# Router products taken from the centred rows, ahead of the variance, in two FFN stages of a fused graph and mixture kernel

## The reference, cut to what matters

```python
def _layernorm(x, axis=-1, eps=1e-05):
    m = jnp.mean(x, axis=axis, keepdims=True)
    v = jnp.var(x, axis=axis, keepdims=True)
    return (x - m) / jnp.sqrt(v + eps)

x = x + _L0_gnn_ref(_layernorm(x), adj, adj, ...)        # attention over the graph, two GRU cells
x = x + _L0_ffn_ref(_layernorm(x)[None], ...)[0]         # shared expert + 8 routed experts, hidden 512, gelu
x = x + _L1_gnn_ref(_layernorm(x), adj, ...)             # bilinear features, adj @ x, relu
x = x + _L1_ffn_ref(_layernorm(x)[None], ...)[0]         # 8 routed experts, hidden 256, relu

# the router of the two FFN layers (first: softmax over all, then renormalised over the two best)
gate_logits = x_flat @ Wg + bg + bias
topk_vals, topk_idx = jax.lax.top_k(gate_logits, 2)
topk_w = jax.nn.softmax(topk_vals, axis=-1)
combine = (jax.nn.one_hot(topk_idx, 8) * topk_w[..., None]).sum(axis=1)
h = relu(einsum('td,edh->teh', x_flat, W1) + b1)
y = einsum('teh,ehd->ted', h, W2) + b2
out = einsum('ted,te->td', y, combine)
```

## Time and profile before

| | us |
|---|---|
| median of 3 runs | 2084.09 |
| the profiled execution's own time | 2085.21 |
| its span, first to last instruction | 2083.4 |
| TensorE busy | 1826.9 (88%) |
| VectorE busy | 1648.8 (79%) |
| ScalarE busy | 1337.1 (64%) |
| GpSimd busy | 221.5 (11%) |
| mean granted TensorE clock | 0.917 |

### The profile page before, as it was taken

How to read it: one execution, slowest core, us unless ns; L and a number is a source line. 1 busy time by engine, 2 the same in 40 slices (tenths; PEclk the granted TensorE clock), 3 DMA queues, 4 the chain that set the end, 5 groups by cost and what they waited for, 6 DMA issues and landing times.

```text
span 2083.4 us, 28364 instructions
## 1 busy us (share of the span) xinstructions
PE 1826.9 (88%) x9108; PEld 875.5 (42%) x9108; DVE 1648.8 (79%) x1393; ACT 1337.1 (64%) x1428; POOL 221.5 (11%) x163
## 2 busy tenths in 40 slices
PE   2511697999999999999998899999999989998997
PEld 2511342444444444444446344444444334455443
DVE  7645777988988998989567687878768988856998
ACT  4766136887887887888234556565546876735775
POOL 2000201000101011000441000000006910000000
PEclk6555798999999999999996999999998999988999
DMA  8998038555555556455500211111002079912321
GB/s 332 407 428 295 24 109 259 152 151 172 151 153 177 148 151 182 137 152 152 206 0 0 94 51 40 50 40 51 1 21 121 0 285 429 422 73 84 112 102 69
DMA packets 89852, 311.84 MB, mean 150 GB/s; under 512 B 15017, under 2 KB 52361, under 8 KB 79903
## 3 DMA queue, kind: packets, MB, share of 16 engines
q1 hardware_dynamic: 89778, 310.88, 42.4%
HBM read 297.88 MB, written 12.98 MB: 149 GB/s over the span
## 4 chain that ended last, share of the span: by engine, by line
PE 53%; DVE 3%; ACT 2%; issue 1%; POOL 0%; ACTq 0%; DVEq 0%; POOLq 0%
PE psum L1119 13%; PE psum L1131 13%; PE psum L1204 8%; PE psum L1067 8%; PE psum L1182 2%; PE psum L1092 1%; PE psum L1094 1%; PE psum L896 1%; PE psum L891 1%; PE psum L1106 1%; DVE prod L1727 1%; PE psum L902 1%; PE psum L1097 1%; PE psum L1096 1%; PE psum L1144 1%
## 5 line engine op out<-in xcount | busy, mean ns | idle before, releaser
L722 ACT ACTIVATE ss<-KR,cls 128x1024 bf16<-128x1024 int16 x384 | 413.0, 1138 | 106.4 <-DVE pl L1562 106.4
L1067 PE MATMUL psum<-ph,Tt 128*128 128x512 bf16 x1536 | 416.4, 380 | 6.7 <-DVE pl L1562 6.7
L800 ACT ACTIVATE hid<-psum,fB 128x1024 f32<-128x1024 f32 x208 | 227.4, 1112 | 184.3 <-PE psum L1119 184.2
L1119 PE MATMUL psum<-hTp,fW 128*128 (+1 forms) x1248 | 290.1, 383 | 7.7 <-ACT hid L800 3.8
L1131 PE MATMUL psum<-hidp,fW 128*128 128x512 bf16 x1248 | 280.1, 379 | 1.9 <-DVEq L1693 1.9
L1559 DVE TENSOR_TENSOR ph<-ss,Ahi 128x3072 bf16<-128x3072 bf16 x128 | 228.6, 1786 | 54.8 <-PE psum L1067 54.7
L1671 DVE TENSOR_TENSOR hidp<-hid,hidp 128x1024 bf16<-128x1024 f32 x208 | 245.5, 1222 | 26.6 <-ACT hidp L794 26.0
L1067 PEld LDWEIGHTS psum<-ph,Tt 128*128 128x128 bf16 x1536 | 149.9, 98 | 190.5 <-DVE pl L1562 7.1
L1067 PE MATMUL psum<-pl,Tt 128*128 128x512 bf16 x768 | 228.9, 380 | 0.0
L1562 DVE TENSOR_TENSOR pl<-ss,Alo 128x3072 bf16<-128x3072 bf16 x128 | 227.3, 1776 | 0.0
L1119 PEld LDWEIGHTS psum<-hTp,fW 128*128 128x128 bf16 x1248 | 117.2, 98 | 169.1 <-ACT hid L800 31.8
(11 more groups left out here) (231 smaller groups left out, 2131.4 us busy)
## 6 DMA issues: line engine op xcount, KB each, us to landing
Ar<-in_adjT SPq DMA_DIRECT2D x32, 2048.0 KB, 13.2
Ab<-in_adjT SPq DMA_DIRECT2D x128, 512.0 KB, 3.9
A<-in_adjT SPq DMA_DIRECT2D x32, 2048.0 KB, 10.1
mB<-mk_d SPq DMA_DIRECT2D x64, 512.0 KB, 3.7
Tt<-T_d SPq DMA_DIRECT2D x128, 192.0 KB, 2.3
Tt<-Tn_d SPq DMA_DIRECT2D x128, 64.0 KB, 2.1
T_d<-tb SPq DMA_DIRECT2D x32, 192.0 KB, 1.9
RD<-rden_d SPq DMA_DIRECT2D x12, 512.0 KB, 4.8
```

Source lines behind the costliest of these rows:

```text
L722: last = nc.scalar.activation(ss[s % 2][:, h, :], KR[:, h, rb * RB:(rb + 1) * RB], ACT.Sigmoid, scale=STEP, bias=cls[:, ds(t * HEADS + h, 1)])
L800: nc.scalar.activation(hid[j % HB][:, :], flat[:, j % 2 * CW:j % 2 * CW + CW], func, bias=fB1[:, j:j + 1]).then_inc(act_done[k], 1)
L1067: last = nc.tensor.matmul(psum[:, 2 * h + q, :], Tt[s % AS][:, h, w, :], mv[:, q * CH:(q + 1) * CH], start=fresh and k == 0, stop=False, s ...
L1119: last = nc.tensor.matmul(psum[:, j % 2 * 2 + b, :], fW[0][x][:, j * P:(j + 1) * P], hTp[y][:, ds(q * CW + b * CH, CH)], start=(w == 0), s ...
```

## The change

- TensorE no longer takes the router products from the scaled rows (`hT`) behind the 32 transposes. It takes them from the centred rows (`hc`), in bank 1 of PSUM. In the first stage the products of chunks 0 to 5 stand behind seven of the eight mean products, and those of chunks 6 and 7 between the variance products of chunks 3 and 4. In the second stage chunks 0 to 3 stand behind the mean products, chunks 4 to 7 between the variance products of chunks 3 and 4.
- VectorE multiplies the logits by the row factor right behind the Newton step (one new instruction of 128x256). The two bias additions follow the scaling of all rows.
- VectorE scales four chunks, forms the low halves of the first two, scales the other four, then goes to the selection. The low halves of chunks 2 to 7 stand behind those of the first hidden blocks. TensorE's first up products wait for four scaled chunks and two low halves, its main loop for all low halves.
- ScalarE takes the exponential behind two of the four first activations, not behind all four.

```diff
@@ lt_tensor
+            def routed(chunks):
+                pe.wait_ge(r_in, 96 * (k // 2 + 1))
+                for q in chunks:
+                    pe.wait_ge(lt_centred, NC * k + max(q, 1) + 1)
+                    for t in range(4 * q, 4 * q + 4):
+                        last = nc.tensor.matmul(psum[:, 1, NE * t:NE * t + NE], hc[:, t * P:(t + 1) * P], Wr[:, :],
+                                                start=(t == 0), stop=True, skip_group_check=True)
+                if q == NC - 1:
+                    last.then_inc(r_ps, 1)
             for q in range(NC):
                 if k == 0:
                     pe.wait_ge(g_nin, 2 * NC + (1 if q < 4 else 2))
                     pe.wait_ge(g_used, 2 * q + 4)
                 if k == 2:
                     pe.wait_ge(l_add, q + 1)
+                if k == 0 and q == NC - 1:
+                    routed(range(6))
                 nc.tensor.matmul(psum[:, q, :], mean, xT[:, q * CH:(q + 1) * CH], start=True,
                                  stop=True).then_inc(lt_mean, 1)
+            if k == 2:
+                routed(range(4))
             for q in range(NC):
+                if q == 4 and k != 1:
+                    routed(range((4, 0, 6)[2 - k], NC))
                 pe.wait_ge(lt_squared, NC * k + q + 1)
...
             for t in range(NT):
+                if t == 4 and k != 1:
+                    pe.wait_ge(r_sel, 3 * (k // 2) + 1)
@@ ffn_tensor
-                pe.wait_ge(r_in, 96 * (k + 1))
-                for t in range(NT):
-                    if t % 4 == 0:
-                        pe.wait_ge(ln_done, 3 + NC * 2 * k + t // 4)
-                    last = nc.tensor.matmul(psum[:, 0, NE * t:NE * t + NE], hT[:, t * P:(t + 1) * P], Wr[:, :],
-                                            start=(t == 0), stop=True, skip_group_check=True)
-                last.then_inc(r_ps, 1)
                 pe.sem_inc(down_done[k], hold)
-                pe.wait_ge(f_lo, (NC + 2) * (k + 1))
+                pe.wait_ge(ln_done, 2 + NC * 2 * k + 4)
+                pe.wait_ge(f_lo, (NC + 2) * k + 4)
...
-                pe.wait_ge(r_sel, 3 * k + 1)
                 for e in range(lag):
                     up(0, e)
+                pe.wait_ge(ln_done, 2 + NC * 2 * k + NC)
...
                 pe.wait_ge(r_mk8, 4 * k + 4)
+                pe.wait_ge(f_lo, (NC + 2) * (k + 1))
@@ lt_vector, k = 0 and 2
+                V.tensor_tensor(lg[:, :, :], psum[:, 1, 0:NT * NE].rearrange("p (t e) -> p t e", e=NE),
+                                stat[:, 4, :].unsqueeze(2).to_broadcast([P, NT, NE]), ALU.mult).then_inc(r_sel, 1)
+                for q in range(4):
+                    scaled(q)
+                for q in range(2):
+                    low_rows(f, q)
+                for q in range(4, NC):
+                    scaled(q)
```

More of the change, by code:

```diff
@@ L805, in hidden @@
                             high(q, j)
-                for j in range(HB):
+                for j in range(2):
                     hidden(0, j)
@@ L810, in ffn_scalar @@
                 nc.scalar.activation(rs[:, 3, :], rs[:, 2, :], ACT.Exp).then_inc(r_exp, 1)
+                for j in range(2, HB):
+                    hidden(0, j)
                 for b in range(4):
@@ L1288, in lt_vector, with scaled @@
                 inverse_root(slice(0, NT)).then_inc(ln_normed, 1)
-                for q in range(NC):
+                def scaled(q):
                     xq = slice(q * CH, (q + 1) * CH)
@@ L1292, in lt_vector, with low_rows @@
                     V.tensor_tensor(hT[:, xq], hc[:, xq], psum[:, q, :], ALU.mult).then_inc(ln_done, 1)
+                if k == 1:
+                    for q in range(NC):
+                        scaled(q)
+                    return
+                f = k // 2
+                dve.wait_ge(r_ps, f + 1)
+                dve.wait_ge(ln_normed, 3 + k)
+                V.tensor_tensor(lg[:, :, :], psum[:, 1, 0:NT * NE].rearrange("p (t e) -> p t e", e=NE),
[5 more added lines that the diff above has]
+                for q in range(4, NC):
+                    scaled(q)
+            def low_rows(k, q):
+                c_q = slice(q * CH, (q + 1) * CH)
+                dve.wait_ge(fh_hi, NC * k + q + 1)
+                V.tensor_tensor(hTp[1][:, c_q], hT[:, c_q], hTp[0][:, c_q], ALU.subtract).then_inc(f_lo, 1)
             dve.wait_ge(cst_in, 16)
@@ L1626, in ffn_vector @@
                 dve.sem_inc(hid_lo[k], HB)
[L1627 to L1634, removed]
                 dve.wait_ge(r_sel, 3 * k + 1)
+                c.link(V.tensor_tensor(lg[:, :, :], lg[:, :, :], rb2[:, 0, :].unsqueeze(1).to_broadcast(T), ALU.add))
                 c.link(V.tensor_tensor(lg[:, :, :], lg[:, :, :], rb2[:, 1, :].unsqueeze(1).to_broadcast(T), ALU.add))
@@ L1704, in ffn_vector @@
                     high(0, e)
+                for q in range(2, NC):
+                    low_rows(k, q)
                 with dve.Fori(0, NW - 1) as q:
```

## The result

The changed kernel took 2093.19 us (median of 5 runs, 2091.73 to 2093.79), against 2084.09 us for the kernel before (5 runs). The ratio is 1.0043, with a 95% interval of 1.0032 to 1.0053: slower by about 9 us. The forecast was 2092.6 us. The profiled execution took 2091.73 us, with a span of 2089.9 us against 2083.4.

A forecast was written before the change was run, and what follows sets the result against it. TensorE, with 53% of the chain, was taken to bound the kernel. Loop starts later by 1.8 us (13.6 - 11.8) and 6.7 (18.9 - 12.2) gave +8.5: 2093.7 profiled, 2092.6 on the median's basis; 8-in-10 range 2085 to 2099.

The forecast's parts named there:

- Ahead of T, first stage: Before the first stage's transposes: 64 router products at half clock throughout delay the first transpose by 13.6 us.
- Ahead of T, second stage: Before the second stage's transposes: transfer wait, router products and half clock delay the first transpose by 18.9 us.
- 2.8 us of idle time: Second stage, after the mean products: TensorE waits from 1861.24 to 1864.0 for all six transfers of `r_in`.
- Behind T: First transpose to main loop: 26.3 us instead of 36.8 in the first stage, 25.1 instead of 37.35 in the second.
- TensorE can start the up products when the transposes end, T + 5.5: First stage: up products start 5.5 us after the first transpose, instead of 14.8.
- the exponential follows at once: First stage, after the selection: ScalarE is free, exponential done 14.5 us after the first transpose; before, VectorE waited 6.48.
- The late low halves: Before the main loop: six low halves at 0.61, 3.7 us, decide its start, 2 us over the first stage's weight transposes.
- the third rival: Both main loops start at half clock after TensorE idles: +4.8 us, 2097.5; chance 13%.
- the 1.3 that I had taken off for the table load: First stage's loop start: a table load of 1.28 now lies ahead of the loop, saving 1.3 us more.
- The sum: Whole kernel: +1.8 and +6.7 make +8.5 us, 2093.7 on the profiled execution, 2092.6 on the median's basis.
- The first two rivals: Router products raise or hold the clock: 2067, 8%; full clock for them alone, variance products as before: 2077, 7%.
- the fourth rival: Second stage's products do not wait for the weights: 2.8 us less, half given back by the clock, 2090; chance 10%.

The follow-up runs named there:

- the quarter of the products: Changed kernel with three of four router tiles left out in both stages: 2074.22 us, ratio 0.9951 to the kernel before.
- The credit experiment: Changed kernel with ScalarE's credit for the first two up products ahead of its eight high halves: 2089.79 us, ratio 1.0028 to the kernel before.
- The zeros: Changed kernel with matmuls of zeros on idle TensorE before the first stage's router products and both main loops: 2087.35 us, ratio 1.0016 to the kernel before.

## Why the prediction was right, point by point

*Ahead of T, first stage: right.* 13.6 us forecast, 13.61 measured. Half clock throughout, the start tied to GpSimd's last addition, and the price of a record (0.213 by the quarter of the products) are all shown.

*Ahead of T, second stage: right in kind, 1.2 us too large.* 18.9 forecast, 17.69 measured. The mis-sized term is the wait for the transfers, "2.8 us of idle time": it was 1.72 in the changed profile. Counted from the first relu addition (A), the products started 9.6 us later there (1861.39 - 1851.79), while the trace of before had led me to 10.5. The variance was read at 1134.45 and 1888.10 instead of near 1138.6 and 1891, mostly since A lay 4.2 and 1.7 us earlier in this execution.

*Behind T: 1.4 and 1.1 us too good.* The step that failed is "TensorE can start the up products when the transposes end, T + 5.5". They started at T + 8.2 and T + 8.0. I had read the semaphore `act_done` as a count of activations; its first two credits are given by ScalarE's queue, behind eight copies. With it "the exponential follows at once" failed: VectorE waited 1.6 us. The credit experiment restores most of both (T + 6.3 and T + 5.6, waits of 0.56 and 0.29). What was left in the first stage are the transposes: they took 6.55 us in the changed kernel instead of 5.53, since the granted clock rose only 5.9 us after their start, and not 3.8 as before. The late low halves decided the loop's start as forecast, with 4.84 and 1.95 us of wait on TensorE.

*The loops' starts: the third rival came true.* L to D grew by 1.25 and 1.68 us; set against the 1.3 that I had taken off for the table load, the half clock costs 2.5 and 1.7, 4.2 for the 4.8 that the rival gave. I had given it 13%. The zeros show it. My evidence against it, a pause of 1.39 us before, was from a shorter pause than the 4.84 and 1.95 that the changed order made. But the length of the pause does not decide it alone: in the credit experiment the second loop ran at full clock behind 3.09 us, and the first lost 1.4 us (6.76 - 5.33) instead of 2.5 behind 4.75. So the size of this term is in part chance of the execution. One reading behind the rival's price was off: of the 8.37 us of the first up products 6.0 were at half clock, not half of them. At 0.2 us more for each matmul its 2.4 us for 12 stands all the same.

*The rest of the first loop: 2.55 us missed.* I counted one table load of the loop. It stood in the loop's body and ran in each of three passes; four loads in all became two. The row that would have said it was the count of `ACT_TABLE_LOAD` at L800. The Trainium skill, "ScalarE: Activation LUTs", section "What ACT_TABLE_LOAD costs", would put such a switch at 2.66 us; here each load taken away from the path gave back 2.55/2 = 1.28 us, the load's own time in the rows.

*The sum.* +8.5 forecast, +9.1 by the medians. By terms it would have been +8.5 - 1.2 + 2.5 + 4.2 - 2.55 = +11.5, as the marks say; identical code elsewhere was 5.0 us shorter in the profiled pair and some 2.4 by the medians. So the good fit is in part luck: misses of opposite sign (6.7 us too good behind T and at the loops' starts, 3.75 too bad at the wait and the table loads), and the scatter between executions.

*The first two rivals fall, and so does the fourth.* The clock stood at 0.50 from the first product to the last variance product in the first stage, and from 0.9 us after the first product on in the second. Started at 1.00, by zeros, it fell again within the products. The wait for the weights, which the fourth rival left out, was there with 1.72 us. (By its own terms, 2.8 us less with half of it given back, its sum should have been 2091 and not 2090.) By the rule of the Trainium skill, "TensorE: Matmul & The Clock Gate", section "What's actually happening", read as the busy share of a profile, the clock would have risen. The traces disagree: TensorE was 100% busy for 29 us and stayed at 1.2 GHz.

## What to carry to other kernels

Before you move small matmuls (few columns for each weight load) to another place, look at the granted clock there: the same 64 records cost 8.9 us behind the transposes, where much of them met full clock, and 13.6 in the new place, where in the second stage the variance products behind them, which had run at full clock for 3.2 us, met half clock too. When a chain is shortened, ask of each engine on it what stands in its queue ahead of the instruction that is now due; reordering ScalarE's queue alone gave 15.7 us in the two stages here (20.7 by the medians, of which 5 are unexplained), and moving TensorE's work alone cost 22.6. And count what stands in a loop by its passes: a table load ahead of the loop instead of inside it was worth 2.55 us of the later passes.

## What the runs showed of the hardware that I had not expected

- TensorE stayed at half clock through 29 us of gapless fp32 matmuls, all but one of them with 8 or 1 columns moving, and matmuls of zeros of 512 columns kept it at full clock through the pause of 5.9 us before them. They need no data. Ahead of the router products they delayed nothing (A to the first product was 0.10 us with and without them); ahead of the first loop they cost 0.3 us.
- A pause of 4.84 us before the loop cost 2.5 us after it (7.87 - 5.33), and one of 1.95 us cost 1.7 (4.28 - 2.60). In the credit experiment pauses of 4.75 and 3.09 us at the same places cost 1.4 and nothing. The second loop started at full clock also in executions of other orders (2.37 to 2.60 us from L to D).
- The way to the variance repeated within 0.1 us between first stages of one order (15.67 in all of the old order without zeros, 29.28 in three of the new) and within 0.4 us between second stages (18.61 to 18.85, 35.93 to 36.31), while the part of the program before A of the first stage, with the same code, differed by up to 7.5 us (1101.88 to 1109.33).
